# First cross attention of a two-layer decoder: probabilities formed from a second, key-major score product instead of being transposed

## The reference

```
Q = (x @ Wq.T).reshape(B, xN, 16, 16)
KV = (z @ Wkv.T).reshape(B, zN, 2, 16, 16);  K = KV[:, :, 0];  V = KV[:, :, 1]
attn = jnp.einsum('bqhd,bkhd->bhqk', Q, K) * SCALE
attn = jax.nn.softmax(attn, axis=-1)
O = jnp.einsum('bhqk,bkhd->bqhd', attn, V).reshape(B, xN, DIM)
return O @ Wo.T
```

## Time and profile before

| | us |
|---|---|
| median of three runs | 3470.06 |
| lowest and highest | 3465.08, 3473.06 |
| the profiled execution, first to last instruction (span) | 3436.3 |
| TensorE busy in the span | 3266.1 (95%) |
| VectorE, ScalarE, GpSimd busy | 1887.3, 1649.4, 785.1 |
| the changed stage | 598.3 to 1202.0 of the span |

### The profile page before, as it was taken

The page is one execution under the profiler, slowest core; times in us unless marked ns, Lnnn a source line. Parts: engine busy times, 40 slices in busy tenths (PEclk is TensorE's granted clock), DMA queues, the critical chain, the costliest instruction groups (busy, mean ns, idle before and its releaser), DMA issues. The chain is left out here.

```text
span 3436.3 us, 76398 instructions
## 1 busy us (share of the span) xinstructions
PE 3266.1 (95%) x24682; PEld 2434.1 (71%) x24683; DVE 1887.3 (55%) x5145; ACT 1649.4 (48%) x4614; POOL 785.1 (23%) x854
## 2 busy tenths in 40 slices
PE   8999999999999989999998999999999999998992
PEld 6777776666666666677776776777777777766871
DVE  4555555677777755122222664666666666663433
ACT  4555555666666620122222326666666666652220
POOL 1000000000000000333332210132332332336874
PEclk9999999999999999999999999999999999999996
DMA  8600000300000051211112100010000000025784
GB/s 269 171 0 0 0 0 0 144 11 11 9 11 11 5 166 35 82 31 31 30 28 46 51 0 5 18 44 20 18 15 11 14 13 12 13 81 139 203 230 133
DMA packets 136408, 181.30 MB, mean 53 GB/s; under 512 B 36156, under 2 KB 108601, under 8 KB 135308
## 3 DMA queue, kind: packets, MB, share of 16 engines
q1 hardware_dynamic: 84112, 133.96, 12.6%
q0 software_dynamic: 45760, 26.67, 4.8%
q10 hardware_dynamic: 6460, 19.66, 1.5%
HBM read 116.11 MB, written 103.61 MB: 64 GB/s over the span
## 5 line engine op out<-in xcount | busy, mean ns | idle before, releaser
L1279 DVE TENSOR_REDUCE e_nmx<-PS 128x1 f32<-128x361 f32 x416 | 221.5, 533 | 341.6 <-PE PS L1126 335.6
L1654 ACT ACTIVATE b_p<-PS,b_nmx 100x361 f32<-100x361 f32 x512 | 267.6, 569 | 150.2 <-DVE b_nmx L1743 150.2
L901 POOL DMA_INDIRECT slot_rows<-r_row,r_rows_now x256 | 257.3, 1005 | 336.1 <-DVE e_p L1286 289.7
L1126 PE MATMUL PS<-e_cT,e_qT 128*128 128x361 f32 x832 | 333.5, 483 | 0.0
L1231 ACT ACTIVATE e_pT<-PS 121x384 f32<-121x384 f32 (+1 forms) x416 | 199.4, 480 | 220.1 <-PE PS L1133 220.0
L2678 PE MATMUL PS<-c_wgu,c_tile_xT 128*128 x912 | 290.7, 462 | 7.2 <-issue 6.4
L1133 PEld LDWEIGHTS PS<-ident,e_p 128*121 128x121 f32 x1248 | 197.9, 184 | 96.2 <-ACT e_pT L1231 0.4
L1743 DVE TENSOR_REDUCE b_nmx<-PS 100x1 f32<-100x361 f32 x512 | 243.8, 526 | 39.0 <-PE PS L1499 39.0
L1236 ACT ACTIVATE e_p<-PS,e_nmx 128x361 f32<-128x361 f32 x416 | 232.8, 560 | 36.2 <-DVE e_nmx L1279 36.2
L1506 PEld LDWEIGHTS PS<-ident,b_p 100*121 100x121 f32 x1536 | 188.2, 185 | 63.3 <-ACT b_pT L1638 33.3
L1506 PE MATMUL PS<-ident,b_p 100*121 100x100 f32 x1536 | 223.1, 280 | 8.8 <-ACT b_pT L1638 6.7
(11 more groups left out here) (340 smaller groups left out, 6492.4 us busy)
## 6 DMA issues: line engine op xcount, KB each, us to landing
f_w<-in_f_W SPq DMA_DIRECT2D x64, 384.0 KB, 3.8
slot_rows<-a_empty SPq DMA_DIRECT2D x1, 21504.0 KB, 65.3
f_xg<-slot_rows SPq DMA_DIRECT2D x64, 336.0 KB, 4.0
c_wgu<-in_c_GU ACTq DMA_DIRECT2D x8, 1408.0 KB, 12.0
sum<-X SPq DMA_DIRECT2D x2, 3200.0 KB, 57.4
f_sums<-sum SPq DMA_DIRECT2D x16, 400.0 KB
b_cT<-in_ctx_T SPq DMA_DIRECT2D x32, 181.5 KB, 2.3
e_cT<-in_ctx_T SPq DMA_DIRECT2D x32, 181.5 KB
```

The lines of the kernel that those rows point to most:

```text
L901: pool.indirect_dma_start(out=self.rows, in_=self.row[:, u, :], in_offset=None, out_offset=bass.IndirectOffsetOnAxis(ap=self.rows_now[:, u ...
L1126: sr.fill_done(pe.matmul(sr.at(f"s{m}", ROWS, CTX), qT[:, at:at + ROWS], cT[:, u, 0:CTX], start=True, stop=True), f"s{m}")
L1279: dve.tensor_reduce(nmx[:, m:m + 1], sr.at(f"s{m}", ROWS, CTX), AX.X, ALU.max, negate=True).then_inc(max_ready, 1)
L1654: sr.move_done(act.activation(p[:, g % 2, a, 0:CTX], sr.at(f"s{g}{a}", S, CTX), ACT.Exp, bias=nmx[:, g, a:a + 1]), f"s{g}{a}")
```

## The change

The probabilities are no longer transposed. After the first scores only the maxima are taken (two reductions a group, each over two banks). They are written at column 16 x (1 - r) of each head's 32 in `nmx`, one transpose (`turn_maxima`, named w) puts all four on their rows, and `shift` adds them to the queries: that row of the queries, zero by the parity, now holds the negated maximum. The keys are moved twice, each time with that same row set to one (`mark`, `unmarked`). `turned_scores` then multiplies again, with 121 keys stationary and the 100 queries moving, so that scores less maxima come out with the keys on the rows, and `exponents` takes two exponentials a group of [121 x 600] straight into `pT`. A group's steps are now four: scored at n + 6, shifted at n + 5, turned at n + 4, weighed at n + 3. Scores and turned scores share three pairs of banks, everything else (with the weighed sums `o`, now moved once a group) shares two banks. The start is a turn of its own (`turn(-1, ...)`), and the loop holds two turns, for the two buffers of queries. SyncE's context loads wait for other pieces.

```
--- before.py
+++ after.py
+class Pairs(Ring):
...
+        self.PS, self.first, self.n, self.uses = k.PS, first, n, k.uses
+        self.filled = [k.filled[first + 2 * b] for b in range(n)]
+        self.moved = [k.moved[first + 2 * b] for b in range(n)]
+
+    def plan(self, names):
+        self.bank = {name: n % self.n for n, name in enumerate(names)}
...
-    AHEAD, TURNED, WEIGHED = 4, 3, 2
+    LAST_KEYS = CTX - (CH - 1) * KEYS
+    SCORED, SHIFTED, TURNED, WEIGHED = 6, 5, 4, 3
+    PIECES = [("xT", "k00"), ("q", "k01"), ("r0", "k10"), ("t0", "v00"), ("y0", "v02"), ("r1", "v10"), ("t1", "v12"),
+              ("k11", "y1")]
+    OWN = ("r0", "t0", "y0", "r1", "t1", "y1")
...
-        qT = sb("qT", [128, T, PAR, 2 * S])
-        kT = sb("kT", [128, 2, T, CTX])
+        qT = sb("qT", [128, 2, T, PAR, 2 * S])
+        kT = sb("kT", [128, 2, T, PAR, KEYS * CH])
-        nmx = sb("nmx", [S, GROUPS, TILES_R])
-        p = sb("p", [S, 2, TILES_R, KEYS * CH])
-        pT = sb("pT", [KEYS, 2, TILES_R, CH, S])
+        nmx = sb("nmx", [S, PAR, TILES_R, 32])
+        qS = sb("qS", [128, PAR, S])
+        pT = sb("pT", [KEYS, 2, TILES_R, CH * S])
...
-        sr = Banks(k, 0, 4).plan([f"s{g}{a}" for g in range(GROUPS) for a in range(TILES_R)])
-        tr = Banks(k, 4, 2).plan([f"p{g}{a}" for g in range(GROUPS) for a in range(TILES_R)])
-        ob = Banks(k, 6, 1).plan(["o0", "o1"])
-        mr = Ring(k, 7, 1).plan(["v10", "v12", "xT", "k00", "r0", "t0", "q", "k01", "y0", "v00", "v02", "k10",
-                                 "r1", "k11", "t1", "y1"])
...
+        sr = Pairs(k, 0, 3).plan([f"{a}{group(n, by)}{half}" for n in range(GROUPS)
+                                  for a, by in (("s", SCORED), ("p", TURNED)) for half in range(2)])
...
+        names = [m for n in range(GROUPS) for m in (*PIECES[n], f"w{group(n, SHIFTED)}", f"o{group(n, WEIGHED)}")]
+        mr = Ring(k, 6, 2).plan(names)
...
-                mr.wait_full(sp, "v02", -1)
-                sp.dma_start(cT[:, 0], k.ctx_T[2]).then_inc(ctx_loaded[0], 16)
-                with sp.Fori(0, TURNS - 2) as i:
-                    mr.wait_full(sp, "v12", i)
+                with sp.Fori(0, TURNS - 1) as i:
+                    mr.wait_full(sp, "v02", i - 1)
+                    load(0, i + 1)
+                    mr.wait_full(sp, "k11", i - 1)
                     load(1, i + 1)
...
+                pool.memset(nmx[:], 0.0).then_inc(prepared, 1)
...
-                pool.memset(p[:, :, :, CTX:KEYS * CH], 0.0).then_inc(prepared, 1)
...
+                    for half in range(2):
+                        sr.wait_free(pe, f"s{g}{half}", i)
                     for a in range(TILES_R):
                         rows = slice(32 * a, 32 * a + 32)
-                        sr.wait_free(pe, f"s{g}{a}", t)
-                        sr.fill_done(pe.matmul(sr.at(f"s{g}{a}", S, CTX), qT[rows, tile, r, u * S:(u + 1) * S],
-                                               kT[rows, u, tile, :], start=True, stop=True), f"s{g}{a}")
-                def turn_probs(g, a, t):
-                    tr.wait_free(pe, f"p{g}{a}", t)
-                    sr.wait_moved(pe, t, f"s{g}{a}")
-                    for c in range(CH):
-                        last = pe.transpose(tr.at(f"p{g}{a}", KEYS, CH, S)[:, c, :],
-                                            p[:, g % 2, a, c * KEYS:(c + 1) * KEYS], k.ident[0:S, 0:S])
-                    tr.fill_done(last, f"p{g}{a}")
-
...
+                        last = pe.matmul(sr.one(f"s{g}{a // 2}", a % 2, S, CTX),
+                                         qT[rows, buffer(n, SCORED, par), tile, r, u * S:(u + 1) * S],
+                                         kT[rows, u, tile, r, 0:CTX], start=True, stop=True)
+                        if a % 2:
+                            sr.fill_done(last, f"s{g}{a // 2}")
+
+                def turn_maxima(n, i):
+                    g, (_, j) = group(n, SHIFTED), before(n, i)
+                    mr.wait_free(pe, f"w{g}", i)
+                    sr.wait_moved(pe, j, f"s{g}0", f"s{g}1")
+                    mr.fill_done(pe.transpose(mr.at(f"w{g}", 128, S), nmx[:, g % PAR].rearrange("p a n -> p (a n)"),
+                                              k.ident[0:S, 0:S]), f"w{g}")
+
+                def turned_scores(n, i):
+                    g, (_, j) = group(n, TURNED), before(n, i)
+                    u, tile, r = g // G, g % G // PAR, g % PAR
+                    mr.wait_moved(pe, j, f"w{g}")
+                    for half in range(2):
+                        sr.wait_free(pe, f"p{g}{half}", i)
                     for c in range(CH):
                         for a in range(TILES_R):
+                            rows = slice(32 * a, 32 * a + 32)
+                            last = pe.matmul(sr.one(f"p{g}{a // 2}", a % 2, KEYS, CH * S)[:, c * S:(c + 1) * S],
+                                             kT[rows, u, tile, r, c * KEYS:(c + 1) * KEYS], qS[rows, r, :],
+                                             start=True, stop=True)
+                            if c == CH - 1 and a % 2:
+                                sr.fill_done(last, f"p{g}{a // 2}")
+
+                def weigh(n, i):
+                    g, (_, j) = group(n, WEIGHED), before(n, i)
+                    u, x = g // G, g % G
+                    mr.wait_free(pe, f"o{g}", i)
+                    if x == 0:
+                        mr.wait_moved(pe, (i, i - 1)[u], f"v{u}2")
+                    sr.wait_moved(pe, j, f"p{g}0", f"p{g}1")
...
+                def turn(i, par, this, nxt):
                     for n in range(GROUPS):
...
+                        if ahead(n, SCORED, this, nxt):
+                            scores(n, i, par)
...
+                        for m in PIECES[n]:
+                            if this if m in OWN else nxt:
+                                piece(m, i)
...
+                        if ahead(n, SHIFTED, this, nxt):
+                            turn_maxima(n, i)
...
+                        if ahead(n, TURNED, this, nxt):
+                            turned_scores(n, i)
...
+                        if ahead(n, WEIGHED, this, nxt):
+                            weigh(n, i)
...
                 keep_busy(pe, k, 6, 8)
                 pe.wait_ge(loaded, LOADED)
...
                 pe.wait_ge(prepared, PREPARED)
+                turn(-1, 1, False, True)
+                with pe.Fori(0, (TURNS - 1) // 2) as m:
+                    for par in range(2):
+                        turn(2 * m + par, par, True, True)
+                turn(TURNS - 2, 0, True, True)
+                turn(TURNS - 1, 1, True, False)
...
                 def move_keys(u, t, i):
+                    mr.wait_full(act, f"k{u}{t}", i)
+                    for r in range(PAR):
+                        last = act.activation(kT[:, u, t, r, :], mr.at(f"k{u}{t}", 128, KEYS * CH), ACT.Identity,
+                                              bias=mark[:, r:r + 1], scale=unmarked[:, r:r + 1])
+                    mr.move_done(last, f"k{u}{t}")
...
+                def exponents(n, i):
+                    g = group(n, TURNED)
+                    for half in range(2):
+                        sr.wait_full(act, f"p{g}{half}", i)
+                        sr.move_done(act.activation(pT[:, g % 2, 2 * half:2 * half + 2, :],
+                                                    sr.both(f"p{g}{half}", KEYS, CH * S), ACT.Exp), f"p{g}{half}")
...
+                def move_sums(n, i):
+                    g = group(n, WEIGHED)
+                    move(mr, f"o{g}", i, sums[:, g // G, g % G, :], mr.at(f"o{g}", 128, S))
...
-                def maximum(g, a, t):
-                    sr.wait_full(dve, f"s{g}{a}", t)
-                    dve.tensor_reduce(nmx[:, g, a:a + 1], sr.at(f"s{g}{a}", S, CTX), AX.X, ALU.max,
-                                      negate=True).then_inc(max_ready, 1)
-
-                def move_probs(g, a, t):
-                    tr.wait_full(dve, f"p{g}{a}", t)
-                    tr.move_done(dve.tensor_copy(pT[:, g % 2, a], tr.at(f"p{g}{a}", KEYS, CH, S)), f"p{g}{a}")
+                def maxima(n, half, i):
+                    g = group(n, SCORED)
+                    sr.wait_full(dve, f"s{g}{half}", i)
+                    r = g % PAR
+                    sr.move_done(dve.tensor_reduce(nmx[:, r, 2 * half:2 * half + 2, 16 * (1 - r)],
+                                                   sr.both(f"s{g}{half}", S, CTX), AX.X, ALU.max, negate=True),
+                                 f"s{g}{half}")
+
+                def shift(n, i, par):
+                    g = group(n, SHIFTED)
+                    u, tile, r = g // G, g % G // PAR, g % PAR
+                    mr.wait_full(dve, f"w{g}", i)
+                    mr.move_done(dve.tensor_tensor(qS[:, r, :],
+                                                   qT[:, buffer(n, SHIFTED, par), tile, r, u * S:(u + 1) * S],
+                                                   mr.at(f"w{g}", 128, S), ALU.add), f"w{g}")
 
...
```

(61 more changed lines are left out.)

304 lines of the change are left out of this document (76 added, 228 removed).

## The result

The changed kernel takes 3505.5 us, median of four runs (3501.4 to 3506.5), beside 3471.0 us (3465.1 to 3473.1) of the kernel before; ratio 1.0096, 95% interval 1.0082 to 1.0111. The forecast was 3456.4, with a range of 3432 to 3488.

What follows compares the result with a forecast made beforehand. TensorE, busy 99% in the middle turns, was taken to bound the first cross attention. Turns -10.1, start +4.2 and end -7.8 us sum to -13.7, so 3470.1 becomes 3456.4 us, range 3432 to 3488.

Steps and rivals of the forecast that it cites:

- The turns, -10.1 us: First cross attention's fifteen middle turns: each 35.7 us against 36.37, together 10.1 us less.
- The steady turn, 35.7 us: One full turn of eight steps, summed from bank-order waits between TensorE, ScalarE and VectorE: 35.7 us.
- the one behind the moved queries: In step 1 of a turn, w waits for two moves of queries; expected as the longest wait.
- The transpose w: TensorE's new transpose of the maxima, one a group, taken as 0.14 us.
- the 1.5 us that the blocks leave open: Old turn of 36.3 us: blocks sum to 34.8 us, the remaining 1.5 us read as waits.
- the 31.0 us of work: TensorE's turn after the change by work alone: 31.0 us, 5.3 less, with waits expected to take most of the gain.
- The start, +4.2 us: Stage start before the first full turn: that turn begins at 633.8 instead of 629.6 us, 4.2 later.
- The end, -7.8 us: Last turn and tail, only two groups left to score: 19.0 us against 26.8, 7.8 less.
- (a): Each step's new wait through three engines outlasts what goes: 0.25 us more a step, +18 us, 3488 us; chance 0.21.
- (b): Turned product's loads run in single file: 2.8 us each, +256 us, about 3712 us; chance 0.06.
- (c): Waits in the turns hidden, TensorE stays the bound: 31 us a turn, 85 less, about 3385 us; chance 0.05.
- (d): Clock falls in the turns because TensorE idles: +12 us a turn, some +190 us, 3650 us; chance 0.03.

Runs made afterwards that it cites:

- e10: The unchanged kernel before, run again for a second profile: 3466.6 us, profiled span 3464.8.
- e1: The changed kernel with TensorE's loop over turns written out, the other engines' loops kept: 3484.4 us, ratio to before 1.0040.
- e3: The kernel before with three turns instead of one in each pass of TensorE's loop: 3499.3 us, ratio 1.0077.
- e7: The changed kernel, loop kept, weighing only the first 121 keys, turned product one matmul a head (1160 instructions a pass, output not the reference's): 3463.9 us.
- e11: e9 with TensorE's loop of two turns put back in place of the turns written out: 3479.0 us, ratio 1.0017.
- e12: The kernel before with TensorE's fifteen middle turns written out instead of looped: 3472.3 us, ratio 1.0000.
- e5: e1 without TensorE's own wait for the cleared buffers ahead of the first half turn: 3478.0 us, ratio 1.0017.
- e6: e5 with the users of the two shared banks reordered, the turned product between w and the second piece: 3472.5 us, ratio 1.0002.
- e9: e6 with each step's longer piece first where possible and VectorE shifting queries between its two maxima: 3445.2 us, ratio 0.9917.

## Why the prediction was wrong

**The turns, -10.1 us, in truth +24.5 against e10: the step that failed.** The sum took all fifteen turns as steady ones. The change states that the loop holds two turns, and I costed that at nothing, without a word on what covers it. The jump was short before (0.215 us) only because a pass was short; now six of them took 3.3 to 3.7 us each, waiting for code, with slow steps behind. e1, e3, e7, e11 and e12 show it: long pass with a jump, loss; long code without a jump or a short pass with one, none of that wait. Written out, the turns took 540.4 us, 3.8 less than e10's: without the jumps over a third of the forecast gain.

**The steady turn, 35.7 us: right** (35.8 to 35.9, TensorE busy 89% in e1). In e1 the scores stand behind the exponentials by 0.16 to 0.19 us in six of eight steps, forecast 0.3, and at the turn's end by 0.76; this, and not the one behind the moved queries (0.56), is a turn's longest wait. In the last turn of the loop, steps 0 to 7 measured 4.16, 5.47, 4.46, 3.92, 4.43, 4.47, 3.51 and 5.50, forecast 4.06, 5.51, 4.37, 4.08, 4.20, 4.37, 3.65 and 5.42. The terms, from the turn written out behind the loop (1180.01 to 1215.83):

```profile
L1741 DVE TENSOR_REDUCE b_nmx<-PS 100x2 f32<-100x722 f32 x16 | 14.3, 906 | 11.8 <-PE PS L1545 11.8
L1689 ACT ACTIVATE b_pT<-PS 121x600 f32<-121x600 f32 x16 | 9.8, 668 | 10.5 <-PE PS L1567 10.4
...
L1674 ACT ACTIVATE b_kT<-PS,b_mark,b_unmarked 128x363 f32<-128x363 f32 x8 | 4.8, 652 | 2.8 <-PE PS L1523 2.7
```

0.906, 0.668 and 0.652 us for forecast 0.90, 0.67 and 0.64. The turned product stands 0.82 us ahead of the weighing (795.11 to 795.93) for 0.80: loads of 121 columns in four row groups do overlap. The transpose w was undersized, 0.24 for 0.14; the chain hid it. One reading of the old turn was off as well: the 1.5 us that the blocks leave open were no waits, for TensorE idled 0.27 us a turn in the earlier trace rows. So the 31.0 us of work was too low; e1 measured 32.1 busy.

**The start, +4.2 us, in truth +13.7 against the earlier trace rows (+14.8 against e10): the second step that failed.** TensorE turned x 6.7 us into the stage, forecast 6.05. Scores of group 0 were to start 12.4 us in, behind the moved queries, and started at 16.6; the six steps behind them were to take 23.1 and took 28.5. I had none of the waits of the passed-over entries, which put those scores behind the second keys' move; and the slow clock, expected for x, keys and queries, came back again and again (value chunks at 624.19 and at 633.78 took 2.06 us, in the earlier trace rows 1.12). How the 9.6 us divide between these was not taken apart. The marks I had costed as work under the clearing of v. Their last instruction ended only with it; that cost nothing here, but held ScalarE in e5.

**The end, -7.8 us: nearly right.** To the end of the last addition it took 20.1 us against 26.8 in the earlier trace rows, so -6.7.

**Rivals.** (a) gave a time near the result by another road: neither turned product nor exponential was long. (b) and (c) are out. (d) was held off with 0.03 because the clock stood at 1.00 in the old turns; its price was far too high, but the clock does fall here: behind the jumps (1.3 to 2.3 us lost in the first step each time), and in e7 and e5 without any wait for code ahead. Why it falls in those places and not in their like is open. No rival had the loop in it.

## What to carry to other kernels

A change that makes a loop's pass longer, by unrolling over buffers, has a price of its own: count TensorE's instructions in a pass, loads included, and look at the reads of the instruction queue during the loop; if there are none before and some after, look at how long the loop's branch takes, and try the turns written out. A jump cost 4.7 to 7.5 us here by the turns of the profiles, and 3.5 to 6.6 by the medians of the runs. A wait that is taken from a ring of banks comes back at the next one in order unless something long is put in front of it; e6 took 0.2 us from a turn, and e9, by reordering it further, 1.9 more, 27 us in all. A start forecast from steady durations is too short where every engine waits for another.

## What the runs showed of the hardware

- A taken jump of TensorE's loop took 0.21 us at passes of 912 and 1160 instructions. At 1670, 1930, 2180 and 2730 it took 3.3 to 3.8 us, once 5.1, with a read of the instruction queue inside each long one and inside none of the short. With the granted clock of 0.50 behind it, it cost 4.7 us at 2180 (6.9 in e11) and 7.5 at 2730 in the old kernel.
- Written out, the same code cost nothing (e12, ratio 1.0000), at one read of 16 KB for some 255 instructions of TensorE.
- The granted clock can fall after a wait of 0.76 us, five times in fourteen turns of one profile (e5), and never in the same place of another (e1).
- An instruction of VectorE on two elements a row took 2.57 us while GpSimd cleared a buffer for 2.66 us, and ended with it.
